# A deformable convolution's band: its close kept in PSUM, and a group of spreads put between two sampling rounds

## The reference

```
x = x + gaussian_blur(gn(x))
x = x + gated_silu(gn(x))
x = x + snake_conv(gn(x))
x = x + deformable_conv(gn(x))      # the stage that the change touches
```

```
off = conv2d(x, offset_w, offset_b);  mod = sigmoid(conv2d(x, mod_w, mod_b))
sampled[c, k, p] = bilinear(x[c], p + tap_k + off_k[p])     # outside the image: 0
out[o, p] = sum over c, k of weight[o, c, k] * sampled[c, k, p]
out = out * mean over k of mod + bias
```

## Time and profile before

| | us |
|---|---|
| median of 3 runs | 3042.99 |
| lowest to highest | 3042.19 to 3044.84 |
| the profiled execution, its own time | 3047.33 |
| span of that execution's instructions | 3045.4 |
| granted PE clock, mean over the span | 0.898 of full |

### The profile page before, as it was taken

How to read it: one execution, slowest core, us unless ns; L and a number is a source line. 1 busy time by engine, 2 the same in 40 slices (tenths; PEclk the granted TensorE clock), 3 DMA queues, 4 the chain that set the end, 5 groups by cost and what they waited for, 6 DMA issues and landing times. The chain is left out here.

```text
span 3045.4 us, 98677 instructions
## 1 busy us (share of the span) xinstructions
PE 2440.8 (80%) x44813; PEld 1585.4 (52%) x44813; DVE 1772.7 (58%) x2823; ACT 1530.6 (50%) x1757; POOL 1027.5 (34%) x740
## 2 busy tenths in 40 slices
PE   1774993739999748799999927699994759999998
PEld 0673442527777524355555515477773434555555
DVE  5894656335555464466767661455555535776764
ACT  1222554235555544476666642355555435666665
POOL 0331000035555200555555300455551015545552
PEclk7897996869999869699999968799997778999999
DMA  1577712011111212121221130111113121112221
GB/s 40 161 204 135 110 28 111 3 39 31 30 29 32 84 58 60 50 66 66 68 68 63 51 119 21 31 27 30 30 24 132 26 57 53 66 66 66 69 68 41
DMA packets 219786, 191.40 MB, mean 63 GB/s; under 512 B 77036, under 2 KB 170784, under 8 KB 218784
## 3 DMA queue, kind: packets, MB, share of 16 engines
q1 hardware_dynamic: 219360, 185.02, 22.0%
HBM read 119.96 MB, written 65.01 MB: 61 GB/s over the span
## 5 line engine op out<-in xcount | busy, mean ns | idle before, releaser
L2179 PE MATMUL dense_spread<-dense_cp,kept_spread_yx 32*128 32x512 f32 x2432 | 478.0, 665 | 77.1 <-DVE dense_cp L2338 63.9
L1460 ACT ACTIVATE snake_samp<-snake_s 128x1024 f32<-128x1024 f32 x320 | 321.1, 1023 | 301.8 <-PE snake_s L1390 301.7
L2358 DVE TENSOR_TENSOR dense_hat<-dense_spread,dense_hat 128x1024 f32<-128x1024 f32 x256 | 301.5, 1219 | 235.4 <-PE dense_spread L2179 235.4
L1523 DVE TENSOR_SCALAR snake_hat<-snake_spread 128x1024 f32<-128x1024 f32 x256 | 301.3, 1218 | 207.7 <-PE snake_spread L1368 207.7
L2283 ACT ACTIVATE dense_hat<-dense_spread 128x1024 f32<-128x1024 f32 x256 | 248.6, 1021 | 324.4 <-PE dense_spread L2179 320.2
L1390 PE MATMUL snake_s<-snake_hat,snake_xt 64*64 64x128 f32 x10240 | 338.7, 275 | 19.0 <-ACT snake_samp L1460 18.8
L2229 PEld LDWEIGHTS dense_s<-dense_hat,dense_xt 64*64 64x64 f32 x11264 | 267.4, 133 | 145.2 <-ACT dense_samp L2303 94.3
L2303 ACT ACTIVATE dense_samp<-dense_s 128x864 f32<-128x864 f32 (+1 forms) x384 | 299.3, 834 | 66.2 <-PE dense_s L2229 66.1
L1390 PEld LDWEIGHTS snake_s<-snake_hat,snake_xt 64*64 64x64 f32 x10240 | 286.4, 134 | 85.2 <-issue 42.1
L2229 PE MATMUL dense_s<-dense_hat,dense_xt 64*64 64x108 f32 x11264 | 308.4, 257 | 0.5
L2241 PE MATMUL dense_s<-dense_samp,kept_w_dcn 64*64 64x264 f32 x4608 | 285.0, 388 | 3.6 <-ACT dense_samp L2303 3.6
(11 more groups left out here) (325 smaller groups left out, 3572.0 us busy)
## 6 DMA issues: line engine op xcount, KB each, us to landing
dense_cp<-offs SPq DMA_DIRECT2D x576, 56.0 KB
x<-blur_x SPq DMA_DIRECT2D x16, 1024.0 KB, 5.1
pre<-snake_ob SPq DMA_DIRECT2D x32, 512.0 KB, 4.1
out<-dense_xr SPq DMA_DIRECT2D x64, 256.0 KB, 3.1
gateconv_low<-x SPq DMA_DIRECT2D x24, 512.0 KB, 9.5
dense_cp<-offs SPq DMA_DIRECT2D x256, 48.0 KB
offs<-dcnoff_cm SPq DMA_DIRECT2D x64, 144.0 KB
residual0Silu_x<-x SPq DMA_DIRECT2D x16, 512.0 KB, 9.0
```

The lines of the kernel that those rows point to most:

```text
L1460: act.activation(samp[u % 2][:, :, i * MS:(i + 1) * MS, :, :].rearrange("p b m t h -> p b (m t h)"), sample_at(u, i)[:, :, :], ACT.Copy).t ...
L1523: ins = dve.tensor_scalar(strided(hat[u % 2][:, 0:1], GUARD + (4 * tau + 2 * half) * SW * SR, [[8, 2], [SW * SR, 2], [SR, SW], [1, 8]]), s ...
L2179: return pe.matmul(bank[:, :], k.spread_yx[r, kind, :], cp[u % 2][r, tile, :], start=True, stop=True)
L2358: dve.tensor_tensor(h, p_hat[pair][:, :, :].rearrange("p t (r x) -> p (t r) x", x=W), h, ALU.mult).then_inc(main_ready, 1)
```

## The change

Two things are changed in `dcn_dense`. In `finish`, the product with `mod` goes back into the PSUM tile in which the weighing was summed, and the add of x3 reads that tile in place of `mod`. Since the tile is then read by the add too, round 1 of the next band waits for `out_done` in place of `scale_done`. And in PE's order, `spread_x(u + 1, 1)`, the x spreads of the second group of taps, stands between round 0 and round 1 in place of behind round 1.

```
@@ sample(u, i)
                 elif i == 1:
                     if u > 0:
-                        pe.wait_ge(scale_done, u)
+                        pe.wait_ge(out_done, u)
@@ PE's loop over u
                 sample(u, 0)
-                sample(u, 1)
                 if more:
                     spread_x(u + 1, 1)
+                sample(u, 1)
                 sample(u, 2)
@@ finish(u)
                 m = mod[u % 2][:, :, :].rearrange("p (v r) x -> p v (r x)", v=2)
-                dve.tensor_tensor(m, weigh_at(u)[:, :, 0:2 * PC], m, ALU.mult).then_inc(scale_done, 1)
+                w = weigh_at(u)[:, :, 0:2 * PC]
+                dve.tensor_tensor(w, w, m, ALU.mult).then_inc(scale_done, 1)
                 dve.wait_ge(scale_done, u + 1)
                 dve.wait_ge(x3_ready, u + 1)
-                dve.tensor_tensor(xr[u % 2][:, :, :], mod[u % 2][:, :, 0:W], xr[u % 2][:, :, :], ALU.add).then_inc(out_done, 1)
+                x = xr[u % 2][:, :, :].rearrange("p (v r) x -> p v r x", v=2)
+                dve.tensor_tensor(x, w.rearrange("p v (r x) -> p v r x", r=2)[:, :, :, 0:W], x, ALU.add).then_inc(out_done, 1)
```

## The result

The changed kernel takes 3107.2 us (median of 6 runs, 3106.6 to 3108.5) against 3043.4 for the kernel before: a ratio of 1.0211, 95% interval [1.0197, 1.0224]. It is 63.8 us slower. The forecast was 3102, or 59 us slower.

What follows compares the result with a forecast made beforehand. PE, busy for 80% of 3045.4 us, was taken as the bound. 58 intervals at 0.98 us (57) plus 1.8 for the last bands gave 59 us more, a median of 3102 us; range 3070 to 3118.

Steps and rivals of the forecast that it cites:

- The x group waits for the copies: On PE behind round 0, the moved pairs wait for ACT's two y copies, until T+1.17 and T+2.09.
- Round 1 is late: On PE, round 1 starts only at T+3.15, where round 2 started before: one round, 0.74 us, late.
- Round 3 waits for round 1's copy: On PE, round 3 reuses round 1's bank, waits for its copy to T+5.08, and starts at T+5.13.
- Something comes back: Earlier x products spare the third last spread its wait: 0.41 us regained, round 4 near T+7.10.
- The last product sets the next band: DVE's L2363 follows ACT's L2288 at T+7.85; the next band's first y group waits for it, to T+8.65.
- The price put on the signal: Between the end of DVE's last product and PE's next y group, the signal takes 0.12 us.
- The band: A band in `dcn_dense` lasts 16.78 us against a mean of 15.80: 0.98 more, 57 us over 58 intervals.
- The last band with a successor: At each group's end, weighing waits for copy 5, adding 0.9 us per group, 1.8 in all.
- The close costs nothing: In `finish`, product and add through PSUM add nothing; even 1.4 us more at the upper bound would be covered.
- The clock: PE's clock stays at 1.00, adding nothing; a rival, chance 0.05, had pauses lower it, costing up to 98 us: 3200.
- the wait for `out_done`: On PE before round 1, waiting for T+0.50 instead of T-0.23 costs nothing, as round 1 begins far later.
- the last one of the sum: Final step: the profiled execution, 3047.3, becomes 3106; the runs' median, 4.3 below it, becomes 3102.

Runs made afterwards that it cites:

- experiment 3: Changed kernel with the second pair's y copy of the second group made by DVE instead of ACT: 3080.7 us, ratio 1.0124.
- experiment 4: Changed kernel with the moved x group one round earlier still, ahead of round 0, directly behind the y group: 3172.2 us, ratio 1.0425.
- experiment 5: Changed kernel with the y group issued two taps of the weighing earlier, x group where the change put it: 3054.7 us, ratio 1.0041.
- experiment 2: Changed kernel with the old order of PE, leaving the close in PSUM and the wait for `out_done`: 3044.4 us, ratio 1.0003.
- experiment 1: Kernel before with the moved x group alone, old close and wait kept: 3106.1 us, ratio 1.0211.
- experiment 8: Kernel before with its first x group one tap of the weighing later, four taps ahead instead of three: 3019.2 us, ratio 0.9926.
- experiment 7: Changed kernel with the moved x group's pairs apart, first behind round 0, second behind round 1: 3103.0 us, ratio 1.0199.
- experiment 9: Experiment 8 with the close in PSUM and the wait for `out_done` added, against the kernel before: 3021.1 us, ratio 0.9933.

## Why the prediction was right

- *The x group waits for the copies.* Forecast T+1.17 and T+2.09 for its pairs; the trace has T'+1.18 (2921.83) and T'+2.09 (2922.74). Experiments 3, 4 and 5 moved the gate or the cover and the band followed: by -0.40 for -0.40, by +0.79 for one round of 0.74, and back by 0.89 for the cover of two taps.
- *Round 1 is late.* Forecast T+3.15; the trace has 3.15.
- *Round 3 waits for round 1's copy.* Forecast T+5.13; the trace has 5.14, with 0.27 in brackets.
- *Something comes back.* The three last spreads take 1.14 instead of 1.55, and round 4 comes at T'+7.10, as forecast.
- *The last product sets the next band.* Forecast T+7.85 for its start and T+8.65 for the y group; the trace has 7.84 and 8.68. The price put on the signal (0.12) was 0.03 too low.
- *The band.* 16.78 forecast, 16.79 measured; the mean of the kernel before was 15.80. Over 58 intervals that is 57.4 us, as forecast (57). The last band with a successor was to add 0.9; it lasts 14.79 instead of 13.92.
- *The close costs nothing.* Right in the bands (experiment 2). The product takes 0.72 in place and the add 0.69.
- *The clock.* It stayed at 1.00. Experiment 4 shows how near the other case was.

One step was missed: the wait for `out_done` was put at nothing. It isn't nothing in the last band of each group. There no spreads stand between round 0 and round 1 and the close comes right behind the weighing, so round 1 waits for the add. PE's timeline:

```profile
1780.28 0.92 PE L2229 MATMUL dense_s<-dense_hat,dense_xt 64*64 64x108 f32 x32
1782.03 1.71 PE L2229 MATMUL dense_s<-dense_hat,dense_xt 64*64 64x108 f32 x64 [0.82 <-DVE dense_xr L2374]
```

That makes the last interval 11.02 us instead of 10.37, 0.65 in each group or 1.3 in all. Experiments 1 and 2 part it from the order: with the old close and wait the interval stays 10.37, with the new ones and the old order it is 11.01. With it the sum in `dcn_dense` is 57.4 + 1.7 + 1.3 = 60.4 us.

The two profiled executions differ by 59.2 in span and by 3107.17 - 3047.33 = 59.8 in time, so the forecast of their difference, 59, was closer than that of the medians, 63.8. The step between the two was the last one of the sum: the profiled execution before lay 4.3 above the median of the runs, and the prediction took as much off for the changed kernel. Its profiled execution lies at its median (3107.17 and 3107.2). Why the kernel before varies more isn't shown; its bands differ from one another (15.67 to 16.25 us), the changed kernel's don't. The interval of the ratio is 8 us wide, so the 3 us between 60.4 and 63.8 can't be told from nothing.

How much of the kernel before's own time was stagger was not in the prediction at all. Its first sentences called PE the bound because it was busy for 15.67 of 15.67 us. The argument didn't need that, since it rested on when each thing started, but read as a statement on the kernel it was wrong: experiment 8 takes 0.43 us out of the mean band of 15.82 by moving one tap.

## What to carry to other kernels

When work that waits for another engine is moved forward in an in-order queue, ask when its input is ready, not when the queue gets to it: all that no longer stands ahead of it no longer hides the wait, and everything behind it is late by that much, plus what their own consumers then add. Write the order down with starts and ends of one band, and check what releases each start; here that gave the new band to 0.02 us. And read an engine's busy share with care where ends are modelled: pairs that could start together and don't are a loss that it doesn't show, and starting them together was worth 0.7%.

## What the runs showed of the hardware

- Two matmuls of 32 rows, on two of the four groups of 32 rows of the array, hold PE for as long as four on all of them: 1.06 us between starts (experiment 7, 2935.03 to 2936.09) against 1.07 for four (changed kernel, 2919.58 to 2920.65). Where the second pair started later than the first, the next work started later by the whole distance: 0.45 apart gave 1.51 us (kernel before, 2921.15 to 2922.66), 0.91 apart 1.97 (changed kernel, 2921.83 to 2923.80).
- An add with both inputs in SBUF that ran beside POOL's L2158, a product with its inputs in SBUF, ended 0.54 to 0.55 us behind it, whatever the overlap, and took up to 2517 ns (experiment 8, 56 adds). With one input in PSUM, and the product before it written to PSUM, the add took 690 to 692 ns beside the same instruction (experiment 9, 56 adds). The product written in place in PSUM took 0.72 us against 0.71 into SBUF.
- A pause of 1.11 us in every band of PE, among shorter ones, went with a lower granted clock for a part of one band in four or five, at 1.3 us each (experiment 4). With pauses of 0.2 to 0.3 us, and one of 1.11 near the end of a group, it stayed at 1.00 (changed kernel).
